# Moving one multiply per chunk and the short convolution's weights from VectorE to GpSimd in the first stage of a two-layer kernel

## The chip, the cores and the metric

The kernel runs on one core of a Trainium2 chip. The metric is the device time of one execution in microseconds (us), given as the median of several runs.

## What is computed

Two layers are computed on 2 sequences of 1024 tokens with 128 features. Layer 0 is an RWKV time mixing followed by a linear layer with fp8 rounding; layer 1 is a gated long convolution followed by a mixture of eight experts. Each part ends in a layer norm. The change touches the RWKV recurrence and the short convolution of layer 1:

```python
def step(carry, kv):
    num, den, mx = carry
    ck, cv = kv
    max_out = jnp.maximum(mx, ck + tf)
    e1 = jnp.exp(mx - max_out)
    e2 = jnp.exp(ck + tf - max_out)
    out = (e1 * num + e2 * cv) / (e1 * den + e2)
    max_st = jnp.maximum(mx + td, ck)
    e1s = jnp.exp(mx + td - max_st)
    e2s = jnp.exp(ck - max_st)
    return ((e1s * num + e2s * cv, e1s * den + e2s, max_st), out)
...
for j in range(D_CONV):
    xc = xc + conv_w[None, :, j, None] * xp[:, :, j:j + Lq]
```

The kernel divides the output's numerator and denominator by `e1`, so that one exponential `E = e2 / e1` is left: `out = (num + E * v) / (den + E)`. The four taps of the short convolution are folded into the projection: for every tap the input weights are multiplied by `conv_w`, and TensorE accumulates four matmuls.

## The kernel before

The first stage (`block` with the tiles `bankA`) walks over chunks of 256 tokens of both sequences, so that a tile is 128 features by 512 tokens. `CHUNKS` is 4, and each engine's function `one(c)` is called for c = 0 to 5: at step c the recurrence works on chunk c, the output projection, the first norm and the fp8 linear layer on chunk c - 1, and the second norm and the input projection of layer 1 on chunk c - 2. Every engine has its own instruction stream in the order written; semaphores connect them.

At a step c VectorE runs `maxima(c)` (the running maximum, lines 787 to 796), `residual_mid(c - 1)` (statistics of the first norm), `scans(c)` (lines 798 to 806: a multiply and four scans for `num` and `den`), `output(c)`, `rounded(c - 1)` (the fp8 rounding, lines 414 to 419, whose last line lets TensorE run `lin`), `output_end(c)` (whose last multiply, L820, gives `rwkv_ready`) and `residual_end(c - 1)`. The output is made in four steps, L812 to L815: `dn = E + den`; `ta = E * v`; the reciprocal of `dn`; `ta = ta + num`. The tile `ta` is the tile `rwkv`, and `dn` is the tile `e2v`, which is why these names stand in the rows. After the output of chunk 0, `conv_weights()` (L781) makes `wconv` with four multiplies.

ScalarE makes the exponentials: L557 for the state, L559 and L561 for `E` (the semaphore `exp_out`), and it copies the keys and values out of PSUM. TensorE projects keys, values and receptances (`project`, L600 to L605), multiplies by the output weights (L654, L655), turns tiles, runs the fp8 linear layer (`lin`, L643), the short convolution (`project_time`, L197), and at steps 0 and 1 the spectra of the long filter (L700). GpSimd only computes the inverse root and the shift of both norms, on tiles of 128 by 4 (`factors`, L723 and L724), for the first norm of chunk c - 1 and then the second.

The second stage (from about 139 us on) is the mixture of experts with the rest of the long convolution; the change has no line in it.

The lines that the change touches, as they stand before:

```python
rec.go(dve.tensor_tensor(pair(dn[:, :]), pair(expo[:, 2, :]), prev(den, c), ALU.add))
rec.link(dve.tensor_tensor(ta[:, :], expo[:, 2, :], vsb[:, :], ALU.mult))
rec.go(dve.reciprocal(dn[:, :], dn[:, :]))
rec.go(dve.tensor_tensor(pair(ta[:, :]), pair(ta[:, :]), prev(num, c), ALU.add))
```

`go` counts an instruction, `wait` waits until all counted ones have ended, and `link` is both.

Of the kernel before, what the change touches and what calls it, by code (L numbers as in the profile page):

```python
# [36 lines left out]
TAPS = 4  # L37
# [140 lines left out]
def two_layers(nc, x_tok, x_feat, vecs, bias8, rows, bcast, biasE, w_a, w_b, k_time, d_skip, w_c, w64, w32, const, consts, out):  # L178
    ds = bass.ds
    with ExitStack() as keep:  # L180
# [184 lines left out]
        with ExitStack() as st:  # L365
# [85 lines left out]
            exp_state = sem("exp_state")  # L451
            exp_out = sem("exp_out")
            scans_done = sem("scans_done")
            rwkv_ready = sem("rwkv_ready")
            wo_done = sem("wo_done")
            var1, var2 = sem("a_var1"), sem("a_var2")
# [253 lines left out]
            @block.gpsimd  # L710
            def _(pool):
                pool.memset(hT[:, :, 0:1], 0.0).then_inc(columns_set, 1)
                pool.memset(neghalf[:, :], -0.5)
                pool.memset(der[:, DTOP:DTOP + 1], RATIO_TOP)
                pool.memset(mx[:, :, 0:1], -1e38)
                pool.memset(num[:, :, 0:1], 0.0)
                pool.memset(den[:, :, 0:1], 0.0)
                pool.memset(h2T[:, :, 0:TAPS - 1], 0.0).then_inc(columns_set, 1)
                pool.wait_ge(columns_set, 2)

                def factors(scratch, ready):
                    stats, mv, ve, rstd, shift = scratch
                    power.link(pool.tensor_tensor(rstd[:, :], ve[:, :], neghalf[:, :], ALU.pow))  # L723
                    pool.tensor_tensor(shift[:, :], shift[:, :], rstd[:, :], ALU.mult).then_inc(ready, 1)  # L724

                def one(c):
                    if valid(c - 1):
                        pool.wait_ge(var1, c)
                        after(pool, x1_ready, c - 1)
                        factors(norms[0], rstd1)  # L730
                    if valid(c - 1):
                        pool.wait_ge(var2, c)
                        after(pool, x2_ready, c - 1)
                        factors(norms[1], rstd2)

                power = Steps(pool, power_steps)
                turns(pool, one)
                pool.wait_ge(b_var, 1)
                pool.tensor_tensor(normB[3][:, :], normB[2][:, :], neghalf[:, :], ALU.pow).then_inc(b_rstd, 1)

            REC, MID, END = 6, 13, 10

            @block.vector
            def _(dve):
# [30 lines left out]
                    dve.wait_ge(b_in, 3 * 16)  # L775
                    dve.tensor_tensor(kt[0:1, 0, :], kt[0:1, 0, :], dskip[:, :], ALU.add).then_inc(taps_ready, 1)

                def conv_weights():

                    for tap in range(TAPS):  # L780
                        dve.tensor_tensor(wconv[:, tap, :], wb[:, W_IN:W_IN + INNER],  # L781
                                          bconv[:, tap * INNER:(tap + 1) * INNER], ALU.mult).then_inc(conv_mixed, 1)

                rec, mid, end = Steps(dve, rec_steps), Steps(dve, mid_steps), Steps(dve, end_steps)

                def maxima(c):
# [21 lines left out]
                def output(c):  # L808
                    dve.wait_ge(exp_out, c + 1)
                    dve.wait_ge(scans_done, 2 * BATCH * (c + 1))  # L810
                    after(dve, wo_done, c)
                    rec.go(dve.tensor_tensor(pair(dn[:, :]), pair(expo[:, 2, :]), prev(den, c), ALU.add))  # L812
                    rec.link(dve.tensor_tensor(ta[:, :], expo[:, 2, :], vsb[:, :], ALU.mult))
                    rec.go(dve.reciprocal(dn[:, :], dn[:, :]))
                    rec.go(dve.tensor_tensor(pair(ta[:, :]), pair(ta[:, :]), prev(num, c), ALU.add))  # L815

                def output_end(c):
# [30 lines left out]
                def one(c):  # L848
                    if valid(c):
                        maxima(c)  # L850
                    if c == 0:
                        linear_weights()
                    if valid(c - 1):
                        residual_mid(c - 1)
                    if c == 0:
                        scans(c)
                        taps()
                        output(c)
                        output_end(c)
                        conv_weights()  # L860
                    elif valid(c):
                        scans(c)
                        output(c)
                        rounded(c - 1)
                        output_end(c)
                        residual_end(c - 1)
                    if c == CHUNKS:
                        products(dve, 0, 0, (psk, psv))
                        rounded(c - 1)
                        split(bef[:, :], be2split[0:3 * EXPERTS, :], cst[:, C_PM:C_PM + 3], late_split)  # L870
                        residual_end(c - 1)
                        products(dve, 0, 1, (psk, psv))
                    if c == CHUNKS + 1:
                        def gates():
                            gate(dve, 0, 0, psf)
                            gate(dve, 0, 1, psk)

                        products_now(dve, 1, 0, (psr, pso), gates)
                        residual(dve, 0, psv)
                        long_norm(dve, 0)  # L880
                        products_late(dve, 1, 0, (psr, pso))
# [737 lines left out]
```

## Time and profile before

| what | value |
|---|---|
| median of 3 runs | 487.36 us (486.51 to 487.36) |
| profiled execution, its own time | 488.38 us |
| its span | 486.6 us |
| busy: TensorE / VectorE / ScalarE / GpSimd | 88% / 67% / 39% / 4% of the span |
| mean granted TensorE clock | 0.962 |

The span is the time from the first to the last instruction; the execution's own time has 1.8 us around it. The busy shares are means over both stages. In rows, PE is TensorE, DVE VectorE, ACT ScalarE and POOL GpSimd; PEclk is the share of full clock that was granted.

### The profile page before, as it was taken

To read this page: it belongs to the slowest core of one execution; us is meant where nothing else is said; L and a number is where in the kernel's file an instruction comes from. 1 tells how busy PE (TensorE), PEld (TensorE's weight loads), DVE (VectorE), ACT (ScalarE), POOL (GpSimd) and SP (SyncE) were. 2 spreads that over 40 slices of the span, in tenths; PEclk is the share of its full clock that TensorE was granted. 3 is DMA by queue.
4 is the path that set the end of the run, shared out by engine and by line. 5 is a ranking of instruction groups with operands and counts; after the bars stand their busy time and mean duration, and the time that the engine had idled before them with its cause. 6 is when DMAs were issued, how large, how long until landed. Compare 5 with 4: busy or idle time off the path is not lost.

```text
span 486.6 us, 4142 instructions
## 1 busy us (share of the span) xinstructions
PE 426.3 (88%) x1392; PEld 207.3 (43%) x1392; DVE 328.0 (67%) x663; ACT 189.9 (39%) x307; POOL 20.5 (4%) x35
## 2 busy tenths in 40 slices
PE   4963898799979959999999999999999999999942
PEld 2331565566825435344544444335534333342310
DVE  4999898799646953596988685574636842642543
ACT  1342757533154311445234355252056535325211
POOL 0010211100000000000000000000000000000000
PEclk9996998989999979999999999999999999999977
DMA  6300000120000000000000000000000000000000
GB/s 231 118 1 1 1 0 1 41 100 1 0 2 2 0 0 1 0 1 0 2 0 0 1 5 16 2 0 0 0 1 0 24 0 1 0 0 1 0 22 22
DMA packets 5152, 7.27 MB, mean 15 GB/s; under 512 B 1080, under 2 KB 4236, under 8 KB 4876
## 3 DMA queue, kind: packets, MB, share of 16 engines
q1 hardware_dynamic: 3972, 4.80, 2.9%
q10 hardware_dynamic: 1160, 2.21, 1.2%
q8 instruction: 11, 0.18, 0.2%
q14 instruction: 9, 0.07, 0.1%
HBM read 5.95 MB, written 1.05 MB: 14 GB/s over the span
## 4 chain that ended last, share of the span: by engine, by line
PE 53%; DVE 8%; issue 5%; ACT 4%; POOLq 0%; POOL 0%; DVEq 0%; ACTq 0%
PE ring L1199 19%; PE ring L1178 7%; PE specbank L253 4%; PE ring L1194 4%; PE ring L1180 4%; PE ring L1207 2%; PE timebank L265 2%; PE ring L1220 2%; PE ring L1224 1%; PE ring L1221 1%; PE timebank L274 1%; DVE hm L1385 1%; PE ring L1213 1%; PE ring L1190 1%; PE ring L1215 1%
## 5 line engine op out<-in xcount | busy, mean ns | idle before, releaser
L1199 PE MATMUL ring<-hm,wc 128*128 128x512 f32 x240 | 108.3, 601 | 0.0
L1199 PEld LDWEIGHTS ring<-hm,wc 128*128 128x128 f32 x240 | 44.0, 190 | 63.0 <-issue 55.5
L197 PE MATMUL bankA<-wconv,h2w 128*128 128x256 f32 x128 | 34.0, 412 | 5.1 <-ACT h2w L568 5.1
L1385 DVE SCALAR_TENSOR_TENSOR hm<-xtm,cst,h 128x512 f32<-128x512 bf16 x48 | 33.3, 746 | 7.4 <-ACT h L1300 7.4
L1313 ACT ACTIVATE gts<-ring 128x512 f32<-128x512 f32 x16 | 9.6, 597 | 52.7 <-PE ring L1199 52.7
L1300 ACT ACTIVATE h<-ring,vec 128x512 f32<-128x512 f32 x32 | 21.9, 687 | 18.1 <-PE ring L1180 15.7
L197 PEld LDWEIGHTS bankA<-wconv,h2w 128*128 128x128 f32 x128 | 24.7, 203 | 9.5 <-ACT h2w L568 5.8
L1458 DVE SCALAR_TENSOR_TENSOR f2e<-hl,f2e 128x512 f32<-128x512 f32 x8 | 5.5, 691 | 32.9 <-ACT hl L1341 32.9
L1194 PE MATMUL ring<-hm,wc 64*128 64x512 f32 x80 | 22.6, 641 | 0.3 <-DVE hm L1385 0.3
L265 PE MATMUL timebank<-cst,abc 128*128 128x256 f32 x96 | 22.6, 394 | 0.0
L1213 PE MATMUL ring<-xn,wc 128*128 128x512 f32 x16 | 10.8, 762 | 12.8 <-DVE xn L1453 12.6
L265 PEld LDWEIGHTS timebank<-cst,abc 128*128 128x128 f32 x96 | 19.1, 200 | 5.3 <-issue 2.7
L1310 ACT ACT_TABLE_LOAD x8 | 10.3, 1283 | 28.4 <-PE ring L1199 28.4
L1178 PE MATMUL ring<-zs,wc 128*128 128x512 f32 x40 | 20.6, 598 | 0.0
L1180 PE MATMUL ring<-zs,wc 128*128 128x512 f32 x40 | 20.4, 592 | 0.0
L1334 ACT ACTIVATE hf<-ring,vec 128x512 f32<-128x512 f32 x16 | 10.4, 674 | 22.3 <-PE ring L1213 19.3
L1434 DVE SCALAR_TENSOR_TENSOR al<-al,zs 128x1536 f32<-128x1536 f32 x4 | 7.0, 1757 | 17.6 <-ACT al L1328 17.6
L253 PE MATMUL specbank<-xtm,cst 128*128 128x512 f32 x40 | 18.5, 605 | 0.0
L1178 PE MATMUL ring<-xtm,wc 128*128 128x512 f32 x40 | 17.9, 595 | 0.0
L1428 DVE TENSOR_TENSOR sps<-sps,dmx 128x1536 f32<-128x1536 f32 x4 | 7.0, 1759 | 11.4 <-ACT sps L1324 11.3
L1310 ACT ACTIVATE sps<-ring 128x512 f32<-128x512 f32 x16 | 9.6, 597 | 12.2 <-PE ring L1199 12.1
L1207 PE MATMUL ring<-hsh,ws 64*128 64x512 f32 x40 | 13.5, 641 | 0.0
(256 smaller groups left out, 754.9 us busy)
## 6 DMA issues: line engine op xcount, KB each, us to landing
wc<-in_w_c SPq DMA_DIRECT2D x1, 1664.0 KB, 7.0
cst<-in_const ACTq DMA_DIRECT2D x1, 1096.0 KB
out<-xall SPq DMA_DIRECT2D x8, 128.0 KB, 1.9
wc<-in_x_feat SPq DMA_DIRECT2D x1, 768.0 KB, 12.1
bconv<-in_bcast SPq DMA_DIRECT2D x1, 512.0 KB, 6.6
wc<-in_k_time ACTq DMA_DIRECT2D x1, 512.0 KB
wc<-in_x_feat ACTq DMA_DIRECT2D x1, 256.0 KB, 3.6
wa<-in_w_a SPq DMA_DIRECT2D x1, 256.0 KB, 3.5
```

The source lines that it names most:

```text
L197: pe.matmul(at, h2w[:, n, h * P + tap:h * P + tap + P], wconv[:, tap, :], start=(tap == 0), stop=False)
L253: ins = pe.matmul(banks[ri][:, :].rearrange("p (b c) -> p b c", b=BATCH), cst[:, C_FWD + kh * 2 * WIN + (2 * ri + e) * P:][:, 0:P], xtm[:, ...
L265: ins = pe.matmul(dst[:, b * WIN:(b + 1) * WIN], z[:, e, at, b * INNER + cc * P:b * INNER + (cc + 1) * P], cst[:, C_INV + (2 * ri + e) * W ...
L1178: ins = pe.matmul(dst[:, :], wc[:, at:at + P], x3T(c) if rnd == 0 else xs(c), start=True, stop=(rnd == 0))
L1180: ins = pe.matmul(dst[:, :], wc[:, at + more:at + more + P], vs(c), start=False, stop=True)
L1194: pe.matmul(dst[:, :], wc[lo:lo + HID, W_E2 + part * P:W_E2 + (part + 1) * P], hm[lo:lo + HID, seat(j, MIXED), :], start=False, stop=False)
L1199: ins = pe.matmul(dst[:, :], wc[:, at:at + P], hm[:, seat(j, made + g - 1), :], start=False, stop=(g == PAIRS - 1))
L1207: pe.matmul(dst[:, :], ws2[lo:lo + HID, part * P:(part + 1) * P], hsh[lo:lo + HID, :], start=True, stop=True).then_inc(S["full"], 1)
L1213: ins = pe.matmul(dst[:, :], wc[:, W_F1:W_F1 + P], xn[:, :], start=True, stop=True)
L1300: act.activation(h[:, e - 1, :], src[:, :], ACT.Gelu, bias=vec[:, V_BE1 + e - 1:V_BE1 + e]).then_inc(S["kept"], 1)
L1310: act.activation(sps[p][:, slot, :], src[:, :], ACT.Softplus).then_inc(S["kept"], 1)
L1385: dve.scalar_tensor_tensor(hm[:, seat(j, k), :], picked, cst[:, C_EG + g:C_EG + g + 1], h[:, g, :], ALU.is_equal, ALU.mult).then_inc(S["hm ...
```

## The change

GpSimd makes `ta = E * v` in each of the four chunks, between its factors of the first and of the second norm, and signals `ta_ready`; VectorE waits for it only ahead of L815's addition. The reciprocal now follows `dn` directly. GpSimd also makes the four tiles of `wconv`, at step 1, behind its multiply of chunk 1. VectorE's `conv_weights` is gone.

```diff
+            ta_ready = sem("ta_ready")
...
@@ gpsimd, one(c), between factors(norms[0], rstd1) and factors(norms[1], rstd2)
+                    if valid(c):
+                        pool.wait_ge(exp_out, c + 1)
+                        pool.wait_ge(kv_copied, c + 1)
+                        after(pool, wo_done, c)
+                        pool.tensor_tensor(ta[:, :], expo[:, 2, :], vsb[:, :], ALU.mult).then_inc(ta_ready, 1)
+                    if c == 1:
+                        pool.wait_ge(b_in, 3 * 16)
+                        pool.wait_ge(q_in, 4 * 16)
+                        for tap in range(TAPS):
+                            pool.tensor_tensor(wconv[:, tap, :], wb[:, W_IN:W_IN + INNER],
+                                               bconv[:, tap * INNER:(tap + 1) * INNER], ALU.mult).then_inc(conv_mixed, 1)
@@ vector
-            REC, MID, END = 6, 13, 10
+            REC, MID, END = 5, 13, 10
...
-                def conv_weights():
-
-                    for tap in range(TAPS):
-                        dve.tensor_tensor(wconv[:, tap, :], wb[:, W_IN:W_IN + INNER],
-                                          bconv[:, tap * INNER:(tap + 1) * INNER], ALU.mult).then_inc(conv_mixed, 1)
...
                     dve.wait_ge(scans_done, 2 * BATCH * (c + 1))
-                    after(dve, wo_done, c)
-                    rec.go(dve.tensor_tensor(pair(dn[:, :]), pair(expo[:, 2, :]), prev(den, c), ALU.add))
-                    rec.link(dve.tensor_tensor(ta[:, :], expo[:, 2, :], vsb[:, :], ALU.mult))
+                    rec.link(dve.tensor_tensor(pair(dn[:, :]), pair(expo[:, 2, :]), prev(den, c), ALU.add))
                     rec.go(dve.reciprocal(dn[:, :], dn[:, :]))
+                    dve.wait_ge(ta_ready, c + 1)
                     rec.go(dve.tensor_tensor(pair(ta[:, :]), pair(ta[:, :]), prev(num, c), ALU.add))
...
@@ vector, one(c)
                         output_end(c)
-                        conv_weights()
```

VectorE's order from the scans of chunk 0 to the maxima of chunk 1, before:

```order
L805 SCALAR_TENSOR_TENSOR den<-expo,den 128x256
L776 TENSOR_TENSOR wc<-wc,dskip 1x256 [waits b_in]
L812 TENSOR_TENSOR e2v<-expo,den 128x512 [waits scans_done,exp_out]
L813 TENSOR_TENSOR rwkv<-expo,vsb 128x512
L814 RECIPROCAL e2v<-e2v 128x512 [waits a_recurrence_steps]
L815 TENSOR_TENSOR rwkv<-rwkv,num 128x512
L819 SCALAR_TENSOR_TENSOR e2v<-thr,e2v 128x512 [waits a_recurrence_steps]
L820 TENSOR_TENSOR rwkv<-rwkv,e2v 128x512 [waits a_recurrence_steps]
L781 TENSOR_TENSOR wconv<-wb,bconv 128x256 x4
L790 SCALAR_TENSOR_TENSOR mx<-der,mx,ksb 128x256 [waits k_copied]
```

And the same place in the changed kernel, whose line numbers are its own:

```order
L811 SCALAR_TENSOR_TENSOR den<-expo,den 128x256
L788 TENSOR_TENSOR wc<-wc,dskip 1x256 [waits b_in]
L817 TENSOR_TENSOR e2v<-expo,den 128x512 [waits scans_done,exp_out]
L818 RECIPROCAL e2v<-e2v 128x512 [waits a_recurrence_steps]
L820 TENSOR_TENSOR rwkv<-rwkv,num 128x512 [waits ta_ready]
L824 SCALAR_TENSOR_TENSOR e2v<-thr,e2v 128x512 [waits a_recurrence_steps]
L825 TENSOR_TENSOR rwkv<-rwkv,e2v 128x512 [waits a_recurrence_steps]
L796 SCALAR_TENSOR_TENSOR mx<-der,mx,ksb 128x256 [waits k_copied]
```

The multiply into `rwkv` and the four into `wconv` have left the row, and the reciprocal stands directly behind the addition of `den`.

GpSimd's order from its first 128x4 work on is now this (before, it had only the pairs of `rstdA` and `shiftA`):

```order
L736 TENSOR_TENSOR rwkv<-expo,vsb 128x512 [waits kv_copied,exp_out,columns_set]
L724 TENSOR_TENSOR rstdA<-veA,neghalf 128x4 [waits a_var1]
L725 TENSOR_TENSOR shiftA<-shiftA,rstdA 128x4 [waits a_power_steps]
L736 TENSOR_TENSOR rwkv<-expo,vsb 128x512 [waits wo_done,kv_copied,exp_out]
L741 TENSOR_TENSOR wconv<-wb,bconv 128x256 [waits q_in,b_in]
L741 TENSOR_TENSOR wconv<-wb,bconv 128x256 x3
L724 TENSOR_TENSOR rstdA<-veA,neghalf 128x4 [waits a_var2]
L725 TENSOR_TENSOR shiftA<-shiftA,rstdA 128x4 [waits a_power_steps]
L724 TENSOR_TENSOR rstdA<-veA,neghalf 128x4 [waits x1_ready,a_var1]
L725 TENSOR_TENSOR shiftA<-shiftA,rstdA 128x4 [waits a_power_steps]
```

The multiply of a chunk stands behind the factors of the first norm and ahead of those of the second; the weights stand behind the multiply of chunk 1.

## Rows read from the trace of the kernel before

**Rows 1.** Busy time by stretch: chunk 0, then steps 1, 2 and 3.
```profile
core 0: us, PE busy (x) PEld busy (x) DVE busy (x) ACT busy (x) POOL busy (x), PEclk, DMA share, GB/s
0.00:28.50 28.50, 18.36 (x42) 8.14 (x43) 21.02 (x47) 8.38 (x15) 0.51 (x11) 1.00 0.41 149
28.50:48.80 20.30, 10.71 (x33) 5.17 (x33) 19.63 (x45) 6.38 (x11) 1.78 (x2) 0.77 0.00 1
48.80:70.80 22.00, 20.44 (x85) 12.79 (x84) 19.89 (x46) 14.03 (x26) 3.36 (x4) 0.98 0.00 0
70.80:92.30 21.50, 18.59 (x78) 12.25 (x77) 19.74 (x44) 14.51 (x26) 3.19 (x4) 0.92 0.00 1
```
**Rows 2.** Timeline, VectorE, chunk 0: start us, us, line, out<-in [idle before <-releaser].
```profile
17.64 0.75 DVE L805 TENSOR_TENSOR_SCAN num<-expo,num,e2v 128x256 f32<-128x256 f32 x1
18.31 0.73 DVE L805 TENSOR_TENSOR_SCAN den<-expo,den 128x256 f32<-128x256 f32 x1
...
20.55 0.67 DVE L812 TENSOR_TENSOR e2v<-expo,den 128x512 f32<-128x512 f32 x1
21.15 0.67 DVE L813 TENSOR_TENSOR rwkv<-expo,vsb 128x512 f32<-128x512 f32 x1
21.86 3.35 DVE L814 RECIPROCAL e2v<-e2v 128x512 f32<-128x512 f32 x1
25.13 0.63 DVE L815 TENSOR_TENSOR rwkv<-rwkv,num 128x512 f32<-128x512 f32 x1
...
27.12 1.42 DVE L781 TENSOR_TENSOR wconv<-wb,bconv 128x256 f32<-128x256 f32 x4
28.46 1.39 DVE L790 TENSOR_TENSOR_SCAN mx<-der,mx,ksb 128x256 f32<-128x256 f32 x2
```
**Rows 3.** Timeline, TensorE: the linear layer of chunks 0 to 2, spectra, convolution.
```profile
21.02 3.60 PE L700 MATMUL bankA<-wc,cst 128*128 128x512 f32 x8
...
44.77 0.61 PE L643 MATMUL bankA<-kq,xq 128*128 128x128 bf16 x4 [7.12 <-DVE xq L419]
45.17 5.96 PE L700 MATMUL bankA<-wc,cst 128*128 128x512 f32 x8
...
59.87 1.99 PE L197 MATMUL bankA<-wconv,h2w 128*128 128x256 f32 x8 [1.36 <-ACT h2w L568]
...
66.94 0.40 PE L643 MATMUL bankA<-kq,xq 128*128 128x128 bf16 x4 [0.20 <-DVE xq L419]
...
88.40 0.40 PE L643 MATMUL bankA<-kq,xq 128*128 128x128 bf16 x4 [0.52 <-DVE xq L419]
```
**Rows 4.** Timeline, ScalarE: the exponential of chunk 0's output.
```profile
17.46 0.72 ACT L561 ACTIVATE expo<-expo,der 128x512 f32<-128x512 f32 x1
```
**Rows 5.** Timeline, GpSimd: factors of the norms.
```profile
34.93 0.47 POOL L724 TENSOR_TENSOR shiftA<-shiftA,rstdA 128x4 f32<-128x4 f32 x1
48.97 1.38 POOL L723 TENSOR_TENSOR rstdA<-veA,neghalf 128x4 f32<-128x4 f32 x1 [13.56 <-DVE veA L158]
50.42 0.60 POOL L724 TENSOR_TENSOR shiftA<-shiftA,rstdA 128x4 f32<-128x4 f32 x1
54.62 1.01 POOL L723 TENSOR_TENSOR rstdA<-veA,neghalf 128x4 f32<-128x4 f32 x1 [3.59 <-DVE veA L158]
55.70 0.38 POOL L724 TENSOR_TENSOR shiftA<-shiftA,rstdA 128x4 f32<-128x4 f32 x1
...
93.49 0.20 POOL L724 TENSOR_TENSOR shiftA<-shiftA,rstdA 128x4 f32<-128x4 f32 x1
```
**Rows 6.** Timeline, VectorE: what it ran beside those factors, and its wait for chunk 3.
```profile
34.69 0.72 DVE L805 TENSOR_TENSOR_SCAN den<-expo,den 128x256 f32<-128x256 f32 x1
...
50.22 0.75 DVE L793 SCALAR_TENSOR_TENSOR expo<-mx,der 128x512 f32<-128x512 f32 x1
50.88 0.69 DVE L794 TENSOR_TENSOR expo<-ksb,mx 128x512 f32<-128x512 f32 x1
...
55.33 0.69 DVE L802 TENSOR_TENSOR e2v<-expo,vsb 128x512 f32<-128x512 f32 x1 [0.79 <-ACT expo L557]
...
94.53 0.89 DVE L151 BATCH_NORM_STATS2 statsA<-bankA 128x6 f32<-128x128 f32 x4 [2.20 <-PE bankA L655]
```

## Prediction

> **What bounds the kernel now.** I first cut the span into stretches by step of the first stage [rows 1]. In the 20.3 us of step 1 VectorE is busy 19.63 us and TensorE 10.71 us; in steps 2 and 3 VectorE is busy 19.89 of 22.0 us and 19.74 of 21.5 us, TensorE 20.44 us and 18.59 us. So VectorE's chain sets the pace up to about 49 us, and from there TensorE and VectorE take turns. I then read TensorE's timeline where it depends on VectorE, at the fp8 linear layer [rows 3]. Ahead of the linear layer of chunk 0 it has stood idle for 7.12 us, waiting for the rounding (L419); ahead of those of chunks 1 and 2 it waits only 0.20 and 0.52 us for the same line. Behind these it has work that needs nothing from VectorE. After chunk 3 VectorE in its turn waits 2.20 us for TensorE [rows 6]. What VectorE saves up to the rounding of chunk 0 therefore moves everything behind it; what it saves later moves at most 0.20 and 0.52 us, while what it loses later moves everything, because then TensorE is the one that waits.
>
> **What VectorE saves.** The multiply L813 starts at 21.15 us, the reciprocal at 21.86 us, and the addition ahead of both at 20.55 us [rows 2]. With the multiply gone, the reciprocal starts where the multiply did, plus the same drain of 0.04 us for the link (21.86 less 21.15 and 0.67): 21.26 us instead of 21.86, a saving of 0.60 us, four times 2.40 us. The four multiplies into `wconv` start at 27.12 us and the maxima behind them at 28.46 us: 1.34 us. In all VectorE loses 3.74 us of work, in front of a chain that is never idle between 27 and 48 us. The two added waits on VectorE cost nothing by themselves if GpSimd is in time.
>
> **Whether GpSimd is in time.** `E` of chunk 0 is finished at 18.18 us [rows 4], and the addition that needs `ta` starts at 25.13 us, now 24.5 us [rows 2]. GpSimd has 6.3 us for a multiply, with the rest of the scans, the addition of `den` and then 3.35 us of reciprocal as cover. At step 1 it is busy with the factors until 35.40 us [rows 5] and has about 5.4 us. The multiply of 128x512 would have to take over 5 us to be waited for. The weights stand behind it on GpSimd's queue and ahead of the factors of the second norm, which are asked for at 48.97 us [rows 5]; `wconv` is first read at 59.87 us [rows 3]. All of this is far from late. The semaphore counts `columns_set`, `b_in` and `q_in` were reached by 20 us. I cost it at nothing.
>
> **What it costs beside VectorE.** This is the term that no row prices. GpSimd's rows show that it cannot read freely while VectorE runs [rows 5]: the 128x4 multiply L724 takes 0.20 us at 93.49 us, with VectorE idle, but 0.47, 0.60 and 0.38 us at 34.93, 50.42 and 55.70 us. Each of the three ends at once behind a VectorE instruction with two operands in SBUF [rows 6]: 35.40 us against 35.41, 51.02 us against 50.97, 56.08 us against 56.02. So the two engines exclude each other on something that such an instruction needs, and GpSimd gets in at the next boundary, not at the next long gap. For operands of four columns VectorE's side of that can't be seen: the instruction behind the boundary at 50.97 us takes its usual 0.69 us. What also can be seen is that the hold isn't GpSimd's whole span: the power at 54.62 us runs to 55.63 us, and VectorE's multiply at 55.33 us still takes 0.69 us [rows 5, 6]. It is the reading that excludes.
>
> The new multiplies read 512 columns of two tiles. They are released while VectorE is in the first of four scans [rows 2, 4], each with two SBUF operands, so by these rows GpSimd waits until that scan's end at about 18.35 us and then reads, and the second scan waits for as long as it reads. Call that time D. The lower end is nothing (reading finds gaps, or the exclusion works one way only). The upper end is the slowest 128x512 instruction in the stage, the reciprocal's 3.35 us. The nearest row is VectorE's own multiply, one every 0.60 us, and no row shows GpSimd faster than VectorE. I take twice that, 1.2 us, as an estimate: GpSimd would read both operands through what it shares, one behind the other, where VectorE reads them together.
>
> The Trainium skill (SBUF — State Buffer, Who interferes with whom) says so outright: a VectorE instruction with two SBUF inputs and a GpSimd instruction that reads SBUF take turns, and whichever starts first holds the shared read interface for its whole instruction. It speaks against this change; that GpSimd waits agrees with the rows, while "for its whole instruction" does not hold for the power at 54.62 us. The skill (GPSIMD Engine Reference, Elementwise — side-by-side cycle accounting) has 4497 ns against VectorE's 2293 ns for an addition of 2048 columns; a quarter of it, as an estimate 1.1 us, would put 1.2 us on the sum below in place of 1.7 us.
>
> **The sum**, with D = 1.2 us and half of that for 256 columns:
> - Chunk 0: one hold in the scans, +1.2, less 0.60 saved; then 1.34 saved: -0.74 us at the maxima of chunk 1.
> - Chunk 1: `ta` is held up by the factors and falls in the third scan, +1.2. The first weight multiply waits for the fourth scan's end and delays the addition of `den`, +0.6. The other three run beside the reciprocal, which has one operand, and cost nothing; if that cover were gone they would cost 1.8 us. Less 0.60: +1.2, in all +0.46 us at the linear layer of chunk 0.
> - Chunks 2 and 3: +1.2 - 0.60 each, +1.2 us. VectorE is then the late one in both, so it all counts.
>
> The sum is 4.5 D - 3.74 = +1.66 us. The profiled execution took 488.38 us (span 486.6), so it would take 490.0 us; it stands 1.0 us above the median of 487.36 us, and on the median the forecast is 487.36 + 1.66 = **489.0 us**. Break-even is at D = 0.83 us. A change under 0.2%, some 0.97 us, can't be told from none here; slower by more than that needs D above 1.05 us.
>
> **The rivals.**
> - *No hold on VectorE* (0.30). GpSimd waits its turn but VectorE never does. For it: VectorE's instructions at 50.88 and 55.33 us are not lengthened [rows 6]. Against: GpSimd read four columns there. Then 0.60 + 1.34 + 0.60 = 2.54 us are saved ahead of chunk 0's linear layer, but only 0.20 and 0.52 us at the next two [rows 3], 3.26 us in all: 484.1 us, faster. This is the case on the other side; it decides if D is below 0.6 us.
> - *A short hold*, D between 0.6 and 1.0 us, near VectorE's own 0.60 us per multiply (0.20): 4.5 D - 3.74 is -1.0 to +0.8 us, say 487.1 us, no difference that can be told.
> - *GpSimd too slow* (0.04): its multiply takes over 5 us, so that L815 waits, each microsecond beyond it four times over. At 6 us that is up to +2 us on top of the forecast, some 491 us. Nothing in the rows asks for it.
> - *The clock shifts.* TensorE's granted clock is 0.77 in the stretch to 48.8 us; after the idle 7.12 us the eight spectrum matmuls take 5.96 us, at 1.2 GHz for part of it, where they took 3.60 us at full 2.4 GHz [rows 1, 3]. A stretch at 1.2 GHz that starts or ends earlier is worth up to 2.4 us either way. It widens each case and carries no sign.
>
> **How the numbers follow.** The forecast, D from 1.0 to 1.6 us, has 0.46 and gives 488.1 to 490.8 us, mostly slower. Slower by over 0.2% is most of that and the slow GpSimd: 0.44. Within 0.2% are most of the short hold and the forecast's low edge: 0.22. Faster is the case without a hold and a piece of the short one: 0.34. Eight in ten lie between 484.1 less half a microsecond for the clock, 483.6, and D = 1.6 us, 490.8, rounded to 491.0 us.
>
> **What would show it.** In the new profile GpSimd's four 128x512 multiplies should take between 1.2 and 2 us each, with the scan behind each release lengthened from 0.73 to about 1.9 us, its start unchanged; one addition of `den`, that of chunk 1, to about 1.3 us; the reciprocal at 3.35 us and starting 0.04 us behind the addition. The idle time ahead of L643's successors should grow over 0.20 and 0.52 us. If the scans keep 0.73 us, the forecast is wrong and the first rival holds: those idle times are then gone. If VectorE is idle ahead of L815's successor, GpSimd was too slow. If VectorE's other instructions are lengthened a little each, all through GpSimd's time, the two share rather than exclude, and D is what their excess sums to.

## The result and the profile after

The median of the changed kernel is 488.45 us (20 runs, 487.79 to 489.77), that of the kernel before, timed beside it, 487.30 us (20 runs). The ratio is 1.0028, its 95% interval 1.0018 to 1.0037: **slower by 0.28%**, 1.4 us by the ratio (0.9 to 1.8) and 1.15 us by the medians. The profiled execution took 488.51 us with a span of 486.5 us, against 488.38 and 486.6 us.

Busy time by stretch, of the changed kernel (columns as in [rows 1]):

```profile
28.50:48.80 20.30, 11.41 (x32) 5.26 (x31) 19.66 (x42) 7.12 (x14) 8.02 (x8) 0.75 0.00 1
48.80:70.80 22.00, 20.18 (x93) 13.29 (x92) 20.52 (x44) 14.65 (x28) 5.58 (x6) 1.00 0.00 0
```

In step 1 GpSimd is busy 8.02 us instead of 1.78, and VectorE, which has one multiply fewer there, is as busy as before, 19.66 us against 19.63. Over the span it has lost 3.74 us of work and is busy 328.2 us against 328.0. Its timeline shows with what:

```profile
16.90 0.75 DVE L811 TENSOR_TENSOR_SCAN num<-expo,num,e2v 128x256 f32<-128x256 f32 x1
17.57 1.69 DVE L811 TENSOR_TENSOR_SCAN den<-expo,den 128x256 f32<-128x256 f32 x1
19.18 0.72 DVE L811 TENSOR_TENSOR_SCAN num<-expo,num,e2v 128x256 f32<-128x256 f32 x1
...
26.76 1.38 DVE L796 TENSOR_TENSOR_SCAN mx<-der,mx,ksb 128x256 f32<-128x256 f32 x2
...
33.62 0.72 DVE L811 TENSOR_TENSOR_SCAN num<-expo,num,e2v 128x256 f32<-128x256 f32 x1
34.26 1.69 DVE L811 TENSOR_TENSOR_SCAN den<-expo,den 128x256 f32<-128x256 f32 x1
36.05 0.96 DVE L817 TENSOR_TENSOR e2v<-expo,den 128x512 f32<-128x512 f32 x1
37.05 3.35 DVE L818 RECIPROCAL e2v<-e2v 128x512 f32<-128x512 f32 x1
...
55.00 0.72 DVE L811 TENSOR_TENSOR_SCAN den<-expo,den 128x256 f32<-128x256 f32 x1
55.64 1.69 DVE L811 TENSOR_TENSOR_SCAN num<-expo,num,e2v 128x256 f32<-128x256 f32 x1
...
76.83 1.80 DVE L811 TENSOR_TENSOR_SCAN den<-expo,den 128x256 f32<-128x256 f32 x1
```

One scan in each chunk takes 1.69 or 1.80 us where the others take 0.72 to 0.75, and the addition of chunk 1 takes 0.96 us where that of chunk 0 takes 0.67 [rows 2]. These are GpSimd's instructions at the same places:

```profile
17.13 1.59 POOL L736 TENSOR_TENSOR rwkv<-expo,vsb 128x512 f32<-128x512 f32 x1 [16.09 <-ACT expo L562]
...
33.65 1.75 POOL L736 TENSOR_TENSOR rwkv<-expo,vsb 128x512 f32<-128x512 f32 x1
35.36 3.60 POOL L741 TENSOR_TENSOR wconv<-wb,bconv 128x256 f32<-128x256 f32 x4
...
55.01 1.77 POOL L736 TENSOR_TENSOR rwkv<-expo,vsb 128x512 f32<-128x512 f32 x1 [0.66 <-ACT expo L562]
...
76.82 1.26 POOL L736 TENSOR_TENSOR rwkv<-expo,vsb 128x512 f32<-128x512 f32 x1 [1.23 <-ACT expo L562]
```

GpSimd starts its multiply at 17.13 us, while the scan of 16.90 us runs; the scan behind that one starts on time, at 17.57 us, and is the long one. In chunks 1 and 2 the two start almost together, but VectorE first: its scans start at 33.62 and 55.00 us, GpSimd at 33.65 and 55.01 us. These scans take their usual 0.72 us, GpSimd takes 1.75 and 1.77 us, and again the next scan is the long one. In chunk 3 GpSimd starts 0.01 us before the scan (76.82 against 76.83 us): there GpSimd takes 1.26 us, its shortest, and that very scan takes 1.80 us, the longest. In these four cases the one that started first wasn't held. On TensorE, at the linear layers of chunks 0 to 2:

```profile
43.71 0.61 PE L644 MATMUL bankA<-kq,xq 128*128 128x128 bf16 x4 [7.77 <-DVE xq L419]
...
65.46 0.40 PE L644 MATMUL bankA<-kq,xq 128*128 128x128 bf16 x4 [0.46 <-DVE xq L419]
...
87.40 0.40 PE L644 MATMUL bankA<-kq,xq 128*128 128x128 bf16 x4 [0.93 <-DVE xq L419]
```

These answer to [rows 3]: the idle time for VectorE's rounding grew from 0.20 to 0.46 us and from 0.52 to 0.93 us. The absolute times are earlier than before because this execution already was: its scan of 16.90 us stood at 17.64 us before [rows 2], 0.74 us later, and nothing that the change touches has run by then. A second trace of the kernel before has that scan at 17.02 us. Such an offset isn't the change's, so what follows counts from there.

### The profile page after: what moved, and what is told of

The parts are those of the page before. It is cut to its first block, busy times and chain, and to the rows that moved or that the text cites. A ratio compares the mean times of both kernels' runs of the same rounds, so it can differ in the third digit from the quotient of the medians.

```text
span 486.5 us, 4146 instructions
## 1 busy us (share of the span) xinstructions
PE 426.5 (88%) x1392; PEld 205.8 (42%) x1392; DVE 328.2 (67%) x655; ACT 190.1 (39%) x307; POOL 30.5 (6%) x43
## 4 chain that ended last, share of the span: by engine, by line
PE 53%; DVE 8%; issue 5%; ACT 4%; POOLq 0%; POOL 0%; DVEq 0%; ACTq 0%
PE ring L1203 19%; PE ring L1182 7%; PE specbank L253 4%; PE ring L1198 4%; PE ring L1184 4%; PE ring L1211 2%; PE timebank L265 2%; PE ring L1224 2%; PE ring L1228 1%; PE ring L1225 1%; PE timebank L274 1%; DVE hm L1389 1%; PE ring L1217 1%; PE ring L1146 1%; PE ring L1194 1%
## 5 line engine op out<-in xcount | busy, mean ns | idle before, releaser
L197 PE MATMUL bankA<-wconv,h2w 128*128 128x256 f32 x128 | 32.9, 402 | 5.1 <-ACT h2w L569 5.1
L265 PE MATMUL timebank<-cst,abc 128*128 128x256 f32 x96 | 21.5, 380 | 0.0
L1182 PE MATMUL ring<-xtm,wc 128*128 128x512 f32 x40 | 19.0, 623 | 0.0
L1114 POOL TENSOR_TENSOR rstdB<-veB,neghalf 128x4 f32<-128x4 f32 x3 | 3.0, 1007 | 187.7 <-DVE veB L158 187.7
```

Of the source, the lines that this page charges most:

```text
L197: pe.matmul(at, h2w[:, n, h * P + tap:h * P + tap + P], wconv[:, tap, :], start=(tap == 0), stop=False)
L265: ins = pe.matmul(dst[:, b * WIN:(b + 1) * WIN], z[:, e, at, b * INNER + cc * P:b * INNER + (cc + 1) * P], cst[:, C_INV + (2 * ri + e) * W ...
L1182: ins = pe.matmul(dst[:, :], wc[:, at:at + P], x3T(c) if rnd == 0 else xs(c), start=True, stop=(rnd == 0))
```

## The experiments

**Theories.** The theory is the prediction's: a GpSimd instruction that reads SBUF while VectorE runs two-operand instructions makes the next of these wait for as long as it reads. Rival A: the time comes from `ta` and the scans sharing tiles (`expo`), or from the added semaphores. Rival B: it goes by GpSimd's busy time, wherever that falls. Rival C: the whole difference is TensorE's clock.

### Which part costs: `ta_only` and `conv_only`

`ta_only` is the change with the weights back on VectorE; `conv_only` is the kernel before with only the weights on GpSimd, where the change has them.

The first, against the change:

```diff
-                    if c == 1:
-                        pool.wait_ge(b_in, 3 * 16)
-                        pool.wait_ge(q_in, 4 * 16)
-                        for tap in range(TAPS):
-                            pool.tensor_tensor(wconv[:, tap, :], wb[:, W_IN:W_IN + INNER],
-                                               bconv[:, tap * INNER:(tap + 1) * INNER], ALU.mult).then_inc(conv_mixed, 1)
...
                         output_end(c)
+                        conv_weights()
```

The second, against the kernel before:

```diff
+                    if c == 1:
+                        pool.wait_ge(b_in, 3 * 16)
+                        pool.wait_ge(q_in, 4 * 16)
+                        for tap in range(TAPS):
+                            pool.tensor_tensor(wconv[:, tap, :], wb[:, W_IN:W_IN + INNER],
+                                               bconv[:, tap * INNER:(tap + 1) * INNER], ALU.mult).then_inc(conv_mixed, 1)
...
-                        conv_weights()
```

> GpSimd makes only ta = E*v, released by the exponential as in the change; VectorE makes the convolution's weights again. Theory (a hold while GpSimd reads): each of the four chunks has one scan of 1.69 us in place of 0.73 us, a hold of 0.96 us against 0.60 us saved, so 4 x 0.36 = +1.4 us against the kernel before: 488.8 us; VectorE's work on the weights is back at 1.34 us. Rival (VectorE's side is as the trace adds it up, but the change's loss comes from the granted TensorE clock, which falls in other places): no fixed relation to the holds, the time stays at the change's 488.4 us or falls back to 487.3 us. Second rival (the loss is in the weights alone, their delay of the den addition and their place on GpSimd's queue): 484.9 us, since ta saves 2.4 us.

> GpSimd makes only the convolution's weights, behind the factors of the first norm at step 1; ta stays on VectorE. Theory: 1.34 us saved on VectorE, and at most three of the four multiplies of 128x256 fall beside instructions with two operands in SBUF, each holding one of them for 0.3 to 0.5 us, so between -0.4 and 0 us: 487.1 us, and every held instruction is one of chunk 1. Rival (no hold, the clock): -1.3 us, 486.0 us. Second rival (weights are the loss): slower than the kernel before.

`ta_only`: 489.96 us (5 runs), ratio 1.0054 [1.0040, 1.0069]. The four scans take 1.69, 1.69, 1.69 and 1.81 us. By its rows the four holds are 3 x 0.96 + 1.08 = 3.96 us, less 4 x 0.60 saved: +1.56 us. Measured are +2.6 us by the ratio. Moving `ta` alone is worse than the whole change.

`conv_only`: 488.44 us (12 runs), ratio 1.0026 [1.0012, 1.0039]. I had expected a small gain, with most of the weights beside the reciprocal. It is a loss. VectorE's timeline of this run at chunk 1:

```profile
33.33 0.72 DVE L805 TENSOR_TENSOR_SCAN den<-expo,den 128x256 f32<-128x256 f32 x1
33.98 1.15 DVE L805 TENSOR_TENSOR_SCAN num<-expo,num,e2v 128x256 f32<-128x256 f32 x1
35.05 1.15 DVE L805 TENSOR_TENSOR_SCAN den<-expo,den 128x256 f32<-128x256 f32 x1
36.29 0.97 DVE L812 TENSOR_TENSOR e2v<-expo,den 128x512 f32<-128x512 f32 x1
37.19 1.21 DVE L813 TENSOR_TENSOR rwkv<-expo,vsb 128x512 f32<-128x512 f32 x1
38.43 3.35 DVE L814 RECIPROCAL e2v<-e2v 128x512 f32<-128x512 f32 x1
```

and GpSimd's:

```profile
33.37 4.48 POOL L735 TENSOR_TENSOR wconv<-wb,bconv 128x256 f32<-128x256 f32 x4
```

Without `ta` ahead of them the weights start 2 us earlier, at 33.37 us, and all four are through at 37.85 us, before the reciprocal starts. There are four multiplies and four lengthened instructions: +0.43, +0.43, +0.28 and +0.54 us, 1.68 us against the 1.34 us saved. In the change only the first of the four meets such an instruction; `ta` pushes the others under the reciprocal. The rows give +0.34 us, the medians +1.24 us, so 0.9 us is left over here too.

### The same work at another moment: `late_ta` and `late_release`

The reciprocal takes 3.35 us and, if the theory holds, shares nothing with GpSimd. `late_ta` is the change with `ta` released when VectorE's addition of `den` is finished; `late_release` also makes two of the weights behind the `ta` of chunk 0 and two behind that of chunk 1.

`late_ta`, against the change:

```diff
                     if valid(c):
+                        pool.wait_ge(rec_steps, c * 5 + 2)
                         pool.wait_ge(exp_out, c + 1)
```

`late_release`, against `late_ta`:

```diff
-                    if c == 1:
+                    if c < 2:
...
-                        for tap in range(TAPS):
+                        for tap in (2 * c, 2 * c + 1):
```

> The change, but GpSimd waits for the addition of den too, so that ta is made beside the reciprocal, which has one operand. Theory: the four scans are back at 0.73 us, 0.96 us less in each chunk; chunk 1 has ta and four weight multiplies, some 4.5 us, beside 3.3 us of reciprocal, so one or two instructions behind it are held, about 0.5 us. Together -2.7 us against the kernel before: 484.6 us. If ta takes over 3.3 us there, VectorE stands idle ahead of the addition of num. Rival (clock or another cost of handing ta over): like the change, about 488.4 us, whatever the place of the multiply.

> As the kernel late_ta, and two of the weight multiplies are moved to chunk 0 and two left in chunk 1, each pair behind ta: 1.26 + 2 x 0.8 = 2.9 us of GpSimd beside 3.3 us of reciprocal. Theory: no VectorE instruction is lengthened anywhere, 0.60 + 1.34 + 0.60 us saved ahead of chunk 0's linear layer, then 0.20 and 0.52 us where TensorE was waiting: -3.3 us against the kernel before, 484.0 us. Rival (clock or handing over): about 488 us.

`late_ta`: 485.45 us (12 runs), ratio 0.9969 [0.9952, 0.9986]. `late_release`: 484.90 us (12 runs), ratio 0.9964 [0.9950, 0.9978], **faster than both kernels**. The two intervals overlap, so which of the two is better isn't shown. Both fell short of what I had expected, -2.7 and -3.3 us: by the medians they gained 1.75 and 2.3 us. The engines do the same work as in the change; only the moment of reading differs. GpSimd in `late_release`:

```profile
20.76 1.27 POOL L737 TENSOR_TENSOR rwkv<-expo,vsb 128x512 f32<-128x512 f32 x1 [19.73 <-DVE e2v L818]
21.98 1.41 POOL L742 TENSOR_TENSOR wconv<-wb,bconv 128x256 f32<-128x256 f32 x2
...
35.19 1.26 POOL L737 TENSOR_TENSOR rwkv<-expo,vsb 128x512 f32<-128x512 f32 x1 [2.16 <-DVE e2v L818]
36.41 1.40 POOL L742 TENSOR_TENSOR wconv<-wb,bconv 128x256 f32<-128x256 f32 x2
```

and VectorE:

```profile
33.58 0.73 DVE L812 TENSOR_TENSOR_SCAN den<-expo,den 128x256 f32<-128x256 f32 x1
34.41 0.69 DVE L818 TENSOR_TENSOR e2v<-expo,den 128x512 f32<-128x512 f32 x1
35.14 3.35 DVE L819 RECIPROCAL e2v<-e2v 128x512 f32<-128x512 f32 x1
38.41 0.63 DVE L821 TENSOR_TENSOR rwkv<-rwkv,num 128x512 f32<-128x512 f32 x1
...
60.08 0.43 DVE L414 TENSOR_SCALAR qm<-q 128x512 uint32<-128x512 uint32 x1 [0.62 <-ACT q L579]
```

All six instructions of GpSimd lie within the two reciprocals, each of 3.35 us as before, and no instruction of VectorE is lengthened. The last row shows where the gain ends: from chunk 2 on VectorE is early and waits 0.62 us for ScalarE. That is why the full 3.74 us of removed work does not come out.

`late_ta` has one hold left. Its four weights run from 36.81 to 40.03 us, past the reciprocal's end at 38.89 us:

```profile
36.81 3.22 POOL L742 TENSOR_TENSOR wconv<-wb,bconv 128x256 f32<-128x256 f32 x4
```

and VectorE shows

```profile
38.81 0.64 DVE L821 TENSOR_TENSOR rwkv<-rwkv,num 128x512 f32<-128x512 f32 x1
39.37 0.94 DVE L414 TENSOR_SCALAR qm<-q 128x512 uint32<-128x512 uint32 x1
```

where L414 takes 0.41 us in the change. So this instruction, which has one operand as the reciprocal has, is held all the same; the number of operands alone doesn't tell what is held.

Rival B falls here: GpSimd is nearly as busy (28.8 and 28.2 us against 30.5 us in the change), and the time is 3.0 and 3.55 us less than the change's. So does the part of Rival A on semaphores, since `late_ta` has one wait more.

### What the hold consists of: four added instructions

These are the kernel before with one unused GpSimd instruction per chunk, into a tile of its own, from a weight tile (`wa`) that nothing writes at that time. They share no tile with VectorE, and VectorE waits for none of them.

`extra_recip` is

```diff
+                    if valid(c):
+                        pool.wait_ge(weights_mixed, 7)
+                        pool.wait_ge(rec_steps, c * 6 + 3)
+                        pool.tensor_tensor(extra[:, :], wa[:, :], wa[:, :], ALU.mult)
```

and `extra_scans` the same with the second wait on `exp_out` for `c + 1`, where `ta` is released in the change. `extra_one` and `extra_half` differ from `extra_scans` in the last line:

```diff
-                        pool.tensor_tensor(extra[:, :], wa[:, :], wa[:, :], ALU.mult)
+                        pool.tensor_scalar(extra[:, :], wa[:, :], 2.0, None, ALU.mult)
```

```diff
-                        pool.tensor_tensor(extra[:, :], wa[:, :], wa[:, :], ALU.mult)
+                        pool.tensor_tensor(extra[:, 0:P], wa[:, 0:P], wa[:, P:2 * P], ALU.mult)
```

> The kernel before, with one more GpSimd multiply of 128x512 f32 per chunk, into a tile that nobody reads, released when the reciprocal starts. VectorE's work is unchanged. Hold theory: the reciprocal has one operand, so nothing waits: 0 us, no VectorE instruction lengthened. Rival (part of the loss of every version so far, some 0.7 us above what their holds sum to, comes with GpSimd working at all beside the others): +0.5 to +1 us with no lengthened instruction. Clock theory for those 0.7 us (TensorE's granted clock, which depends on where its idle time falls, shifts with the first stage's timing): 0 here, since no timing is shifted.

> The same extra multiply, released by the exponential of the output as in the change, so beside the scans. Hold theory: one scan per chunk at 1.7 us in place of 0.73 us, 4 x 0.96 = +3.9 us: 491.1 us, or some 0.7 us more if the shift of the clock comes on top. Rival (the hold is bound to the tiles that both engines read or write, expo, vsb or rwkv, and not to the reading as such): scans at 0.73 us and 0 us, since it reads the weights' tile wa and writes a tile of its own.

> The same place beside the scans, but a multiply by a constant: one operand of 128x512 read. It asks where the 0.96 us comes from. If GpSimd reads its two operands one behind the other and holds for all its reading, the hold is about half, 0.45 to 0.5 us, and a scan takes 1.2 us; if it holds for its whole work, as long as before or as its own span.

> The same place, two operands of 128x128 each: a quarter of the columns. If the hold goes with the columns read, 0.24 us, and one scan per chunk takes 0.97 us; if each GpSimd instruction has a fixed hold, more than that.

| kernel | added instruction | GpSimd's span, us | scan behind it, us | hold, us | time, ratio [95%] |
|---|---|---|---|---|---|
| `extra_recip` | 128x512, two operands, beside the reciprocal | 1.04 | 0.72 | 0 | 487.22, 0.9987 [0.9969, 1.0005] |
| `extra_scans` | the same, at the scans | 1.31 to 1.52 | 1.46 | 0.74 | 490.99, 1.0067 [1.0043, 1.0092] |
| `extra_one` | 128x512, one operand, at the scans | 1.92 to 1.98 | 1.03 | 0.30 | 488.42, one run |
| `extra_half` | 128x128, two operands, at the scans | 0.59 to 0.95 | 0.88 | 0.16 | 487.59, one run |

The rows behind the table's first three lines, GpSimd's of `extra_recip`,

```profile
20.97 1.04 POOL L735 TENSOR_TENSOR extra<-wa 128x512 f32<-128x512 f32 x1 [19.94 <-DVE rwkv L818]
```

VectorE's reciprocal beside it,

```profile
20.83 3.35 DVE L819 RECIPROCAL e2v<-e2v 128x512 f32<-128x512 f32 x1
```

GpSimd's of `extra_scans`,

```profile
17.29 1.31 POOL L735 TENSOR_TENSOR extra<-wa 128x512 f32<-128x512 f32 x1 [16.26 <-ACT expo L562]
```

VectorE's of `extra_scans`,

```profile
17.68 1.46 DVE L810 TENSOR_TENSOR_SCAN den<-expo,den 128x256 f32<-128x256 f32 x1
19.07 0.72 DVE L810 TENSOR_TENSOR_SCAN num<-expo,num,e2v 128x256 f32<-128x256 f32 x1
```

GpSimd's of `extra_one`,

```profile
17.79 1.93 POOL L735 TENSOR_SCALAR extra<-wa 128x512 f32<-128x512 f32 x1 [16.77 <-ACT expo L562]
```

and VectorE's of `extra_one`:

```profile
17.71 0.73 DVE L810 TENSOR_TENSOR_SCAN den<-expo,den 128x256 f32<-128x256 f32 x1
18.35 1.03 DVE L810 TENSOR_TENSOR_SCAN num<-expo,num,e2v 128x256 f32<-128x256 f32 x1
19.31 0.72 DVE L810 TENSOR_TENSOR_SCAN den<-expo,den 128x256 f32<-128x256 f32 x1
```

The pair `extra_recip` and `extra_scans` is the cleanest of the study: one instruction per chunk, moved by 3.7 us in chunk 0, and 4 x 0.74 = 2.96 us between them by the rows, 3.8 us by the medians. No tile is shared with VectorE, so Rival A falls: a hold needs no shared tile and no added wait on VectorE. The hold is 0.74 us here and 0.96 us in the change. That the tiles of the change are shared is hardly the reason, because `conv_only`'s weights come from two tiles that the scans don't touch and hold them 0.43 us for half the columns; a run with two separate unshared tiles of 128x512 wasn't made. `extra_one` shows that the hold isn't GpSimd's span: its instruction lasts 1.93 us, until 19.72 us, and the scan of 19.31 us already runs undisturbed. `extra_half` shows that it goes about with the columns: 0.16 us for a quarter of them, where a quarter of 0.74 is 0.19. I had expected more of both; the one-operand form holds less than half of what the two-operand form does. That the hold is the time in which GpSimd reads fits all of these, but no trace shows the reading itself.

### What the sums leave over: `late_ta_only`, `extra_vector`, and both kernels again

With the holds as measured, the change should cost 4.22 - 3.74 = +0.5 us and `ta_only` +1.56 us; they measured about +1.4 and +2.6 us by the ratio. `conv_only` is 0.9 us above its sum, `late_ta` and `late_release` are each about 1 us above theirs by the medians. Four runs went after that remainder. `late_ta_only` is `late_ta` with the weights back on VectorE, by the same diff as that of `ta_only`. `before_again` and `after_again` are both kernels without an edit. `extra_vector` is the kernel before with one unused multiply per chunk on VectorE, a plain delay with no GpSimd in it:

```diff
                     after(dve, wo_done, c)
+                    dve.tensor_tensor(extra[:, :], wa[:, :], wa[:, :], ALU.mult)
                     rec.go(dve.tensor_tensor(pair(dn[:, :]), pair(expo[:, 2, :]), prev(den, c), ALU.add))
```

> GpSimd makes only ta, released when the reciprocal starts; the weights are back on VectorE. Hold theory: no instruction is lengthened; 0.60 us saved in chunks 0 and 1 each, then at most 0.20 and 0.52 us: -1.2 to -1.9 us against the kernel before. If the 0.7 to 1.2 us by which ta_only, the change, late_ta and late_release all came out above what their holds and savings sum to belongs to moved timing, -0.5 us here; if to the weights' place on GpSimd, the full -1.7 us.

> The kernel before with one more VectorE multiply of 128x512 per chunk, ahead of the addition of den, and nothing on GpSimd: a plain delay of 4 x 0.60 us. By VectorE's chain +2.4 us. If moved timing costs by itself, through TensorE's granted clock, +3.1 us or more; if not, the excess of the other versions has to do with GpSimd's multiplies.

> The kernel before, unchanged: a second trace of it and the spread of the comparison. Expected 0 us, ratio 1.000. Clock theory: the stretch of half clock at about 141 us, which the first trace of this kernel lacks and six of the seven traces of other versions have (1.6 us), is there in this one; if it is absent again, the versions lose it by something they do.

> The change, unchanged: a second trace and a second comparison. Holds of 0.96, 0.96, 0.96 and 1.08 us in the four scans and 0.27 us in one addition, as in the first trace; +0.5 us by VectorE's chain, +1.1 us in the runs so far; the clock theory puts the difference between traces of the same kernel at up to 1.6 us, with the same holds in both.

`before_again`: 487.62 us (12 runs), ratio 1.0015 [0.9993, 1.0036]. `after_again`: 488.23 us (11 runs), 1.0021 [1.0013, 1.0030], with the same holds in its trace (1.70, 1.69, 1.70, 1.80 and 0.96 us). So the sign of the result stands up in a second measurement. The kernel before compared with itself shows no difference that can be told, as it should, but its interval reaches from -0.3 to +1.8 us, which is as wide as the effect.

Part of the difference lies outside the span. Time less span is 2.0 us in every run of the change and 1.8 us in every run of the kernel before whose span is known. In the second comparison the median spans are 486.2 us (change) and 485.5 us (before), +0.7 us where the times give +0.9 us. No run tells what these 0.2 us are; `ta_only`, `late_ta_only`, `extra_recip` and `extra_scans` have them as well, `late_ta`, `late_release` and `extra_vector` don't.

`extra_vector`: 490.42 us (6 runs), 1.0068 [1.0055, 1.0080], so +3.3 us for four multiplies that the rows price at 0.60 us each, 2.4 us. The remainder of nearly 1 us (0.3 to 1.5 us by the interval) is there **without any work added on GpSimd**, so such a remainder needs no hold. It isn't in the profiled execution, which is the fastest of the six (489.98 us). From the first scan of chunk 0 to the end of the span that execution took 471.37 us, and the two of the unchanged kernel took 468.96 and 468.88 us: +2.4 and +2.5 us, as the rows price it. Measured the same way, the two executions of the change took 469.60 and 468.75 us, one above and one below the kernel before. The traces alone therefore don't give the sign of the change; the medians do.

`late_ta_only` missed: 488.23 us (12 runs), 1.0009 [0.9994, 1.0024], where its rows have no hold in them. Its executions fall in two groups, four from 485.61 to 486.30 us and eight from 488.04 to 488.82 us, with none between. The four lie 1.0 to 1.7 us below the median of the kernel before, near the 1.2 to 1.9 us that I had expected. The profiled one is of the eight, and TensorE at the start of the second stage shows

```profile
138.91 1.91 PE L1148 MATMUL ring<-xtm,wrh 128*32 128x512 f32 x2 [0.75 <-ACT xtm L1269]
140.76 6.12 PE L1184 MATMUL ring<-xtm,wc 128*128 128x512 f32 x10
```

The same twelve matmuls of the kernel before, first in the execution of [rows 3], then in that of `before_again`:

```profile
140.74 1.04 PE L1142 MATMUL ring<-xtm,wrh 128*32 128x512 f32 x2 [0.75 <-ACT xtm L1263]
141.72 4.56 PE L1178 MATMUL ring<-xtm,wc 128*128 128x512 f32 x10
```

```profile
139.48 1.06 PE L1142 MATMUL ring<-xtm,wrh 128*32 128x512 f32 x2 [0.75 <-ACT xtm L1263]
140.47 6.19 PE L1178 MATMUL ring<-xtm,wc 128*128 128x512 f32 x10
```

The ten matmuls take 4.56 us in one execution and 6.19 us in the other, with a granted clock of 1.00 and 0.66 in the stretch from 140 to 145 us, for the same program. The changed kernel has 5.62 us in one execution and 4.56 us in the other. Of the nine traces of other versions taken before `before_again`, eight have the slow stretch (not six of seven, as my expectation says); that the unchanged kernel has it too speaks against something that the versions do. Ahead of these matmuls TensorE has stood idle in both executions, 2.81 and then 0.75 us. In `late_ta_only` the twelve take 8.03 us where the kernel before took 5.60 us at full 2.4 GHz: 2.4 us, as much as lies between its two groups. But `before_again` took 7.25 us for them, and against that it is only 0.8 us. That is an argument from single profiled executions, not proof: the executions that weren't profiled don't tell where their slow stretches lie.

At one more place the granted clock differs, and there by version. Take the eight convolution matmuls that follow the output projection of chunk 3. They are, in the kernel before and then in the changed kernel,

```profile
97.44 3.66 PE L197 MATMUL bankA<-wconv,h2w 128*128 128x256 f32 x8 [1.36 <-ACT h2w L568]
```

```profile
96.44 1.99 PE L197 MATMUL bankA<-wconv,h2w 128*128 128x256 f32 x8 [1.36 <-ACT h2w L569]
```

with a granted clock of 0.70 and 1.00 between 96 and 100 us. The second traces have 3.50 and 1.99 us. From the linear layer of chunk 2 to that of chunk 3 the change is 1.0 and 0.8 us shorter for it (17.90 and 17.91 us against 18.91 and 18.74), and 0.5 us of that is lost again up to the second stage (32.56 against 32.06 us). Over all fourteen traces the eight matmuls take 1.99 us in eight and 2.94 to 3.66 us in six. `extra_vector`, the plain delay, is among the eight. So moved timing does change what the clock costs, here in favour of the change, and a sum over VectorE's chain doesn't have it.

Rival C, that the whole difference is the clock, falls: the holds stand in VectorE's rows, repeat in the second trace, and move the time with the moment of reading (`extra_recip` and `extra_scans`). That the clock has a share of the change's own 1.4 us isn't excluded.

## Why the prediction was right

It forecast 489.0 us, slower, +1.66 us on the median; measured were 488.45 us and +0.9 to +1.8 us by the interval. The mechanism is right: where the hold falls, how often, and what escapes it. The size is partly luck, because two misses cancel: the hold was smaller than I took it, and the sum leaves out a term that I had given no sign. With the hold as measured, 0.96 us, my own rivals put this case under *A short hold* (D between 0.6 and 1.0 us), with no difference that can be told.

- **VectorE's saving**, 0.60 us a chunk and 1.34 us for the weights: right. The reciprocal starts 0.03 to 0.04 us behind the addition's end. At the maxima of chunk 1 the sum had -0.74 us; the rows have 26.76 against 28.46 us, less the 0.74 us of offset, -0.96 us. The difference is the size of D.
- **GpSimd in time**: right. GpSimd needs 1.26 to 1.77 us for `ta`, which is finished before the reciprocal even starts (18.72 against 21.49 us, 35.40 against 37.05 us); L820, the addition that reads it, never waits. The price that I gave the rival *GpSimd too slow*, up to +2 us at 6 us, doesn't follow from its own words: four times the 1 us beyond 5 us is 4 us. The estimate that I had worked out from the Trainium skill (GPSIMD Engine Reference, Elementwise — side-by-side cycle accounting), 1.1 us, is a little under the 1.26 us that the multiply takes beside the reciprocal in `late_release`.
- **The hold**: the mechanism is right in place, direction and count: one scan per chunk, its start unchanged, its length grown. The first rival, no hold on VectorE, is refuted by 1.69 us where it needed 0.73. The size was too high: D is 0.96 us three times and 1.07 us once, not 1.2. I had doubled VectorE's own 0.60 us; the true value lies under what GpSimd needs for the whole instruction. The Trainium skill (SBUF — State Buffer, Who interferes with whom) has the turn-taking right, which is what spoke against this change; that a turn lasts for the whole instruction doesn't agree with these runs (0.96 of 1.26 us, 0.30 of 1.93 us).
- **The weights**: one hold of 0.27 us in place of 0.6, and the other three free under the reciprocal, as forecast. The drain of some 0.1 us between the last scan and the addition takes part of it. `conv_only` gives the price of that cover: 1.68 us for four.
- **The sum**: 4.5 D - 3.74 becomes 3 x 0.96 + 1.07 + 0.27 - 3.74 = +0.5 us. By this alone the change would be the second rival, a difference that can't be told. The rest, up to +1.4 us by the ratio, lies in what the sum leaves out: 0.2 us outside the span, and TensorE's clock, which I had taken as a widening without a sign. `extra_vector` shows an excess of nearly 1 us for a moved first stage without GpSimd, so a plain sum of VectorE's chain can leave out a term of that size. I can't say what it is in full. That the slowdown is clear of noise at all hangs on this rest.
- **The idle times** at the linear layers grew over 0.20 and 0.52 us, as they should if VectorE is the late one. With the measured holds the chain can be followed there. The linear layer of chunk 0 should be moved by 2 x 0.96 + 0.27 - 1.20 - 1.34 = -0.35 us, where the prediction had +0.46; from 44.77 to 43.71 us, less the offset of 0.74, it is -0.32. At chunk 2 it should be -0.35 + 0.36 + 0.47 = +0.48 us, and it is -0.26 (88.40 to 87.40 us, less the offset): the eight spectrum matmuls in between took 5.29 us where they took 5.96 [rows 3], and 0.48 - 0.67 is -0.19.
- **The clock**, which the prediction let widen every case, acted in both directions in this one pair of executions: 0.67 us back at the spectra, 1.67 us back at the eight convolution matmuls at about 97 us (of which 0.5 us was left at the start of the second stage), and 1.65 us lost at the start of the second stage, where the twelve matmuls took 1.63 + 5.62 us instead of 5.60.

**What stays open**: how much of the remaining 0.9 us is the clock. Two executions of one program differ by 0.5 and 0.7 us at the spectra and by 1.65 us at the start of the second stage; at about 97 us the versions differ and the executions of one program hardly do. Whether the change shifts how often the slow stretches come, or whether another cause is behind the remainder, no run here decides.

## What to carry to other kernels

Before work goes from VectorE to GpSimd, look at what VectorE runs at the moment when GpSimd will read: beside the scans, a GpSimd multiply here saved VectorE 0.60 us and held it for 0.96 us; beside the reciprocal it cost nothing. The moment is a matter of one semaphore: released one step later, the same change went from 0.28% slower to 0.31% faster (0.14% to 0.48% by the interval), and with the weights split over two reciprocals it is 0.36% faster, not told apart from that. And when a sum over one engine's chain comes out within a microsecond of zero, time a plain delay and the unchanged kernel too: here the delay missed its sum by nearly 1 us, and the unchanged kernel against itself was uncertain by about as much either way.

## What the runs showed of the hardware that I had not expected

- The hold follows operands and columns, not the span of GpSimd's instruction: 0.96 us for 128x512 from two tiles (1.07 us where GpSimd started first), 0.74 us where both operands are the same tile, 0.30 us for one operand, 0.16 us for 128x128 (the last two from one profiled execution each).
- GpSimd's multiply of 128x512 by a constant takes 1.92 to 1.98 us beside the scans, longer than that of two operands at the same place, 1.31 to 1.52 us, although it holds VectorE for less.
- The reciprocal (3.35 us for 128x512) is neither held nor lengthened by a GpSimd multiply, while a `tensor_scalar` of one operand was, 0.94 us in place of 0.41, once in these traces.
- Two executions of one program can differ by 1.6 us in ten matmuls: 4.56 us at a granted clock of 1.00 and 6.19 us at 0.66.
